# Audio tower on one core: attention scores issued round the column groups, states as four 32x32 products, moments on GpSimd, levels by halves, and a new order

## The chip, the cores and the metric

One NeuronCore of a Trainium2 chip runs the whole program. The metric is the device time of one execution in microseconds. The engines are PE (TensorE, matrix products), DVE (VectorE), ACT (ScalarE), POOL (GpSimd) and SP (SyncE, which here only issues DMAs). Everything is fp32.

## The reference, cut to what matters

```python
h = dct(frames(x))                                   # 16 batches x 938 tokens x 128
def attn(x):                                         # lam = exp(-exp(time_decay)), 4 heads of 32
    h = layernorm(x)*g + b;  xx = shifted(h)
    q, k, v, gate = four mixes of (h, xx), each @ W.T
    q, k = exp(rmsnorm(q)), exp(rmsnorm(k))
    A_t = lam*A_{t-1} + k_t v_t^T;  z_t = lam*z_{t-1} + k_t
    att = sigmoid(gate) * (q_t A_t / q_t.z_t) @ Wo.T;  x = x + att
    return x + gelu(layernorm2(x) @ W1.T) @ W2.T
h = h + attn(layernorm(h))
def ffn(x):                                          # expert of batch b is b % 8
    xa = layernorm(x)*g + b;  xa = xa @ attn_w.T + attn_b + x
    return gelu((gelu(xa @ fc1[e].T + b1) @ fc2[e].T + b2) @ next_w.T + next_b)
h = h + ffn(layernorm(h))
```

## The kernel before, in words

A batch has 938 tokens, in 8 tiles of 128 (the last has 42, of which two windows of 32 are computed). Work that fits 512 columns goes by halves: g=0 is tiles 0 to 3, g=1 tiles 4 to 7 (426 columns). Each engine has its own program, a fixed order of steps written out by hand in its `body`; engines meet only at semaphores, and each engine takes its steps strictly in that order. `every_round` calls `body` for B + LAST rounds; `at(late)` gives the batch that a round works on with a lateness, so that `at(0)` is the newest batch and `at(1)`, `at(2)` the ones before it. Products go to eight PSUM banks: five are shared by a list of uses (`USES`, with each use's lateness), and `BETWEEN`, `DIAG` and `SOUT` are held for the attention.

The linear attention with decay is computed in chunks. Within a tile the scores of a query and a key are a product of q and k, each scaled by powers of lam against a common reference point, and this is done by levels, so that no power grows large. `qlev` (L711) writes three scaled copies of q per group g of 256 columns into `qq` (Q8: inside 32, Q32: second half of each 64, Q64: second half of each 128). `inside` (L833) writes eight scaled copies `ki` of k, and `between` (L836) three copies `ko` and two `kw`; both go through `klevels` (L820 to L829), one DVE instruction per copy and group (L827). `spread` (L307) moves `qq` by DMA into the block form `qx`, where each head's rows are kept apart and the rest are zero. A score product thus has 128 rows, 32 stationary columns (keys of one window) and moves 4 heads x n columns.

On PE, per tile c:
- `pairs_a` (L976) fills bank BETWEEN: for each window w the three `ko` products (L990, 4x8 = 32 columns moved), then the two `kw` products of 32 keys (L994, 128 columns), then one with 64 keys (L998, 256 columns).
- `pairs_b` (L1001) fills bank DIAG: for each of 8 positions j, round the windows, one `ki` product (L1014, 16 columns).
- `scan` (L1018) adds in bank SOUT the state that enters the tile (L1029, one full 128x128 product with `ab`, the four heads' states on the diagonal of a block matrix) and the tile's own part (L1033, four products of 32 stationary columns, one per head).

An fp32 product is issued as two PE instructions, each with its own weight load (PEld), so counts of the profile are twice those of the code. The window w, and in L1033 the head, choose the 32 output partitions and thereby the group of 32 columns of the PE array.

ACT copies bank BETWEEN into `px` (`pxs`, L514); DVE then lays the masked bank DIAG over it (`merge`, L756, L763), which `scan` multiplies. `chain` (L752) scans the states `af` on DVE, and POOL's `states` (L393) multiplies them with the head mask into `ab`. Bank and buffer reuse binds them: `pairs_a(c+1)` waits for `pxs(c)`, `pairs_b(c+1)` for `merge(c)`.

The three layer norms are `stats` (L641, DVE), `gathered` (L644 to L647, bn_aggr per tile), a scaling of the variance (L653, L654, L782), a power on POOL (L386, L403, L412), and a normalising pass per tile on DVE (L672, L788, L808). `powq` (L391) is POOL's root for the norms of q and k.

The steps around a batch: `samples`, `dcts`, `hcopy`, norm 1, `nTs`, `hlT`, `shifted`, `mixes`, `qkv`, `squares`, `sums`, `norms`, `tokens`, `qkTs`, `exps`, levels, pairs, `scan`, `gated` (needs `gz`, which `hand_gate` brings by DMA), `attends`, `attended`, norm 2, `n2Ts`, `w1s`, `gelu1` (L533), `w2s` (L1056), `hidden`, norm 3, `nmTs`, `n1Ts`, `ats`, `x_attn`, `f1s` (L1078), `gelu2` (L553), `f2s` (L1084), `fin`, `oTs`, `result`, `store`.

Of the kernel before, what the change touches and what calls it, by code (L numbers as in the profile page):

```python
# [6 lines left out]
ALU = mybir.AluOpType  # L7
# [3 lines left out]
P = 128  # L11
HEADS = 4
# [15 lines left out]
LAST = 2  # L28
USES = [
# [23 lines left out]
def program(nc, A, out):  # L53
# [15 lines left out]
    with ctx:  # L69
# [42 lines left out]
        st1, vv1 = sb("st1", TILES, 6), sb("vv1", TILES, 2)  # L112
        hl = sb("hl", PADT + 1)
# [21 lines left out]
        ab = sb("ab", NST, P)  # L135
# [35 lines left out]
        bn1 = sem("bn1"); ag1 = sem("ag1"); var1 = sem("var1"); nl_ok = sem("nl_ok"); d_ok = sem("d_ok")  # L171
# [5 lines left out]
        x2_ok = sem("x2_ok"); bn2 = sem("bn2"); ag2 = sem("ag2"); var2 = sem("var2"); nl2_ok = sem("nl2_ok")  # L177
        h1_ok = sem("h1_ok"); bn3 = sem("bn3"); ag3 = sem("ag3"); var3 = sem("var3"); nb3_ok = sem("nb3_ok"); n1_ok = sem("n1_ok")
# [3 lines left out]
        t_ok = sem("t_ok"); ab_ok = sem("ab_ok"); kin_ok = sem("kin_ok"); kon_ok = sem("kon_ok")  # L182
# [87 lines left out]
        def _(sp):  # L270
# [927 lines left out]
```

## Time and profile before

| | us |
|---|---|
| median of 3 runs | 1221.79 (1215.12 to 1226.37) |
| the profiled execution | 1218.9 |
| its span | 1217.1, granted clock 0.990 |
| PE busy | 1138.9 (94%) |
| DVE busy | 986.5 (81%) |
| ACT busy | 621.5 (51%) |
| POOL busy | 300.9 (25%) |

The span runs from the first to the last instruction of the profiled execution. A PE instruction counts as busy from its start until its result is written, so closely packed small products overlap in time, and the drain between two of them counts as busy too. What a stretch of PE costs is therefore better read from the starts of its rows.

### The profile page before, as it was taken

The page shows a single profiled execution, that of the slowest core. Times are in us where ns is not written, and L with a number is a line of the kernel's source. Part 1 is how long each engine was busy: PE and PEld are TensorE (multiplying, and loading weights), DVE is VectorE, ACT ScalarE, POOL GpSimd, SP SyncE. Part 2 cuts the span into 40 slices and gives each one's busy share as a digit, 9 for nine tenths or more (in the row PEclk, how much of TensorE's full clock was granted, in tenths as well). Part 3 has the DMA queues.
Part 4 walks back from the last instruction along what each step waited for, and adds up shares of the span by engine and source line. Part 5 has one row for each costly group of instructions (what it writes and reads, how often), then busy time and mean ns, then how long its engine had stood idle before and what let it go on. Part 6 is the DMA issues. An engine that isn't in the chain of part 4 may idle for free.

```text
span 1217.1 us, 43497 instructions
## 1 busy us (share of the span) xinstructions
PE 1138.9 (94%) x17955; PEld 807.8 (66%) x17955; DVE 986.5 (81%) x3362; ACT 621.5 (51%) x1100; POOL 300.9 (25%) x174
## 2 busy tenths in 40 slices
PE   4799999999999999999999999999999999999997
PEld 4576676666767676766666667666676766667664
DVE  7878788797887979788796887979879797987962
ACT  3346446363554736446363554736446364554634
POOL 4123131221403223131311403223131221403211
PEclk8799999999999999999999999999999999999999
DMA  5321313222141312313222141312313222141210
GB/s 188 106 64 39 113 43 110 65 79 56 43 132 44 87 47 66 110 43 113 63 78 55 44 130 46 88 45 63 112 44 110 63 80 57 43 132 45 87 55 17
DMA packets 51492, 91.48 MB, mean 75 GB/s; under 512 B 9536, under 2 KB 26592, under 8 KB 51296
## 3 DMA queue, kind: packets, MB, share of 16 engines
q1 hardware_dynamic: 51296, 88.69, 24.1%
q8 instruction: 144, 2.36, 0.8%
q14 instruction: 52, 0.43, 0.1%
HBM read 19.50 MB, written 9.78 MB: 24 GB/s over the span
## 4 chain that ended last, share of the span: by engine, by line
PE 83%; DVE 9%; POOL 4%; issue 3%; ACT 2%; DVEq 0%; POOLq 0%
PE bank L1056 10%; PE bank L1049 9%; PE bank L1084 9%; PE bank L1078 8%; PE bank L919 8%; PE bank L914 7%; PE bank L1014 7%; PE bank L998 5%; PE bank L990 4%; PE bank L1033 4%; POOL nrm L391 3%; PE bank L1029 3%; PE bank L954 3%; PE bank L943 2%; PE bank L994 2%
## 5 line engine op out<-in xcount | busy, mean ns | idle before, releaser
L514 ACT ACTIVATE px<-bank 128x512 f32<-128x512 f32 (+1 forms) x128 | 72.8, 569 | 218.0 <-PE bank L998 152.9
L763 DVE COPY_PREDICATED px<-mask,bank 128x512 f32<-128x512 uint32 (+1 forms) x128 | 88.6, 692 | 79.6 <-issue 76.8
L1078 PE MATMUL bank<-xa,f1w 128*128 128x512 f32 (+1 forms) x256 | 124.7, 587 | 14.8 <-DVE qtok L704 13.0
L1056 PE MATMUL bank<-w,hid 128*128 128x128 f32 x1024 | 121.9, 277 | 17.2 <-ACT hid L533 17.2
L1056 PEld LDWEIGHTS bank<-w,hid 128*128 128x128 f32 x1024 | 116.7, 192 | 31.6 <-ACT hid L533 31.6
L1014 PEld LDWEIGHTS bank<-qx,ki 128*32 128x32 f32 x7680 | 89.6, 110 | 42.3 <-issue 33.9
L827 DVE TENSOR_TENSOR ki<-k,rp 128x96 f32<-128x96 f32 (+13 forms) x512 | 113.2, 295 | 0.6 <-ACT k L499 0.6
L397 POOL TENSOR_TENSOR ab<-af,heads 128x896 f32<-128x896 f32 x16 | 40.8, 2552 | 291.1 <-DVE af L755 291.1
L1049 PE MATMUL bank<-c,w 128*128 128x512 f32 (+1 forms) x256 | 111.4, 568 | 1.1 <-ACT c L527 0.9
L1084 PE MATMUL bank<-hid,f2w 128*128 128x512 f32 (+1 forms) x256 | 107.5, 563 | 0.0
L1014 PE MATMUL bank<-qx,ki 128*32 128x16 f32 x7680 | 99.2, 193 | 6.9 <-issue 6.6
L408 POOL TENSOR_TENSOR t_sum<-x,hs 128x512 f32<-128x512 f32 x32 | 51.4, 1605 | 214.2 <-DVE x L775 200.8
L391 POOL TENSOR_TENSOR nrm<-ssq,phalf 128x8 f32<-128x8 f32 x32 | 66.6, 2082 | 149.7 <-DVE ssq L691 149.7
L553 ACT ACTIVATE hid<-bank,f1b 128x512 f32<-128x512 f32 (+1 forms) x128 | 81.4, 650 | 40.6 <-PE bank L1078 40.3
L533 ACT ACTIVATE hid<-bank 128x512 f32<-128x512 f32 (+1 forms) x128 | 71.9, 562 | 51.4 <-PE bank L1049 51.4
L990 PE MATMUL bank<-qx,ko 128*32 128x32 f32 x2880 | 79.6, 199 | 3.0 <-issue 2.7
L386 POOL TENSOR_TENSOR hs<-vv,nhalf 128x16 f32<-128x16 f32 x16 | 46.4, 2900 | 127.8 <-DVE vv L654 127.8
L1078 PEld LDWEIGHTS bank<-xa,f1w 128*128 128x128 f32 x256 | 39.8, 189 | 55.8 <-DVE qtok L704 25.4
L686 DVE SCALAR_TENSOR_TENSOR mixed<-d,vec,hl 128x938 f32<-128x938 f32 x64 | 76.0, 1188 | 0.6
L412 POOL TENSOR_TENSOR rr<-vv,nhalf 128x8 f32<-128x8 f32 x32 | 52.4, 1636 | 90.8 <-DVE vv L654 90.8
L990 PEld LDWEIGHTS bank<-qx,ko 128*32 128x32 f32 x2880 | 68.2, 111 | 10.0 <-issue 8.8
L1084 PEld LDWEIGHTS bank<-hid,f2w 128*128 128x128 f32 x256 | 46.2, 190 | 42.1 <-issue 42.1
(142 smaller groups left out, 2414.0 us busy)
## 6 DMA issues: line engine op xcount, KB each, us to landing
qx<-qq SPq DMA_DIRECT2D x256, 96.0 KB
hs<-hs SPq DMA_DIRECT2D x32, 532.0 KB, 4.4
v<-v_f SPq DMA_DIRECT2D x16, 512.0 KB, 3.9
gz<-gate_f SPq DMA_DIRECT2D x16, 512.0 KB, 4.7
xT<-in_xT SPq DMA_DIRECT2D x16, 468.5 KB, 4.0
f1w<-in_fc1T SPq DMA_DIRECT2D x16, 256.0 KB, 2.7
f2w<-g_dram SPq DMA_DIRECT2D x16, 256.0 KB, 3.0
out<-t_sum SPq DMA_DIRECT2D x16, 256.0 KB, 2.7
```

The costliest lines, as they stand in the source:

```text
L391: gp.tensor_tensor(nrm[:, i, :], ssq[:, i, :], phalf[:, :], ALU.pow).then_inc(rr_ok[i], 1)
L553: nc.scalar.activation(hid[:, j, cols(g)], bk(f"f1_{g}{j}")[:, 0:width[g]], ACT.Gelu, bias=f1b[:, b % E, j:j + 1]).then_inc(ge2, 1)
L763: V.copy_predicated(px[c % 2][0:n, :, 0:n], mask[0:n, 0:n].rearrange("p (o m) -> p o m", o=1).to_broadcast([n, HEADS, n]), bank[DIAG][0:n, ...
L827: last = V.tensor_tensor(view(dst[:, GRP * (g % 2):GRP * (g % 2) + w]), view(k[:, GRP * g:GRP * g + w]), over(rp[:, P - ref:P - ref + n], ...
L914: last = mm(dst[:, P * i:P * i + P], src[:, P * m:P * m + P], w[:, :], start=True, stop=True)
L919: last = nc.tensor.transpose(dst[:, P * i:P * i + P], src(m), ident[:, :])
L990: last = mm(O[r, :, WIN * w + t:WIN * w + t + EIGHT], ko[:, j - 1, k0 + WIN * w:k0 + WIN * w + WIN], x[:, :, Q8 + t0 + t:Q8 + t0 + t + EIG ...
L1014: last = mm(D[WIN * w:WIN * w + WIN, :, WIN * w + j:WIN * w + WIN:EIGHT], ki[:, j, k0 + WIN * w:k0 + WIN * w + WIN], x[:, :, t0 + j:t0 + W ...
L1049: mm(dst[:, 0:width[g]], w1[:, P * j:P * j + P], c1[:, cols(g)], start=True, stop=True).then_inc(w1_ok, 1)
L1056: last = mm(dst[:, P * i:P * i + P], hid[:, j, P * m:P * m + P], w2[:, j, :], start=(j == 0), stop=(j == 3))
L1078: mm(dst[:, 0:width[g]], f1w[:, P * j:P * j + P], xa[:, cols(g)], start=True, stop=True).then_inc(f1_ok, 1)
L1084: last = mm(dst[:, 0:width[g]], f2w[:, P * j:P * j + P], hid[:, j, cols(g)], start=(j == 0), stop=(j == 3))
```

## The change

1. `pairs_a` and `pairs_b` become one step `pairs`. The product with 64 keys is two with 32 keys, each 256 columns; the `kw` products come first, then the `ko` products round the windows (w inside j), then `ki` as before. The step waits for both `pxs(c-1)` and `merge(c-1)` at its start.
2. The block matrix `ab` and POOL's `states` go. `scan` multiplies each head's 32x32 state with that head's 32 rows of `qc`: four products per tile on the array's diagonal.
3. The aggregation of the moments and the scaling of the variance leave DVE; POOL does them with six to eight small instructions and waits between them.
4. `qlev`, `inside` and `between` run on 512 columns instead of 256, half as many instructions.
5. LAST is 3, the list of bank uses is new, and the order of every engine's body is new: the round begins in the middle of the batch that was at(0), so that most of the attention is now at(1) and the feed-forward part at(2).

```diff
-LAST = 2
+LAST = 3
...
+        def last_pairs(eng, b, g):
+
+            if g:
+                eng.wait_ge(pb_ok, nth(b, TILES, TILES // 2))
+            else:
+                before(eng, pb_ok, b, TILES, TILES)
...
             def spread(b, g):
-                sp.wait_ge(ql_ok, nth(b, GROUPS, g + 1))
+                sp.wait_ge(ql_ok, nth(b, 2, g // 2 + 1))
...
+            def moments(st, mv, sums, odd, s, up, n):
+
+                gp.tensor_tensor(sums[:, s, :], st[:, s, 1:3], st[:, s, 4:6], ALU.add)
+                gp.tensor_tensor(odd[:, s], st[:, s, 1], st[:, s, 4], ALU.subtract).then_inc(up, 1)
+                gp.wait_ge(up, n + 1)
+                gp.tensor_tensor(odd[:, s], odd[:, s], odd[:, s], ALU.mult)
+                gp.tensor_scalar(mv[:, s, 0], sums[:, s, 0], 0.5, None, ALU.mult).then_inc(up, 1)
+                gp.wait_ge(up, n + 2)
+                gp.tensor_scalar(odd[:, s], odd[:, s], 32.0, None, ALU.mult).then_inc(up, 1)
+                gp.wait_ge(up, n + 3)
+                gp.tensor_tensor(odd[:, s], odd[:, s], sums[:, s, 1], ALU.add).then_inc(up, 1)
+                gp.wait_ge(up, n + 4)
+
+            def twice_normed(vv, odd, s, up, n):
+
+                gp.tensor_scalar(vv[:, s, 0], odd[:, s], 1.0 / P, EPS, ALU.mult, ALU.add)
+                gp.tensor_scalar(vv[:, s, 1], odd[:, s], (1.0 + EPS) / P, EPS * EPS, ALU.mult, ALU.add).then_inc(up, 1)
+                gp.wait_ge(up, n)
+
             def pow1(b):
-                gp.wait_ge(var1, nth(b, 1, 1))
+                all_ = slice(0, TILES)
+                gp.wait_ge(bn1, nth(b, 2, 2))
+                before(gp, hs1_in, b, 16, 16)
+                moments(st1, mv1, sm1, od1, all_, mo1, nth(b, 5, 0))
+                twice_normed(vv1, od1, all_, mo1, nth(b, 5, 5))
...
-            def states(b):
...
-            def gathered(mv, st, ms, ag, count):
...
             def qlev(b, g):
-                dve.wait_ge(eq, nth(b, 2, g // 2 + 1))
+                dve.wait_ge(eq, nth(b, 2, g + 1))
...
+                    last = V.tensor_tensor(qq[:, 2 * g:2 * g + 2, at:at + GRP * n // m].rearrange("p o (x m) -> p o x m", m=n),
+                                           q[:, 2 * g:2 * g + 2, :].rearrange("p o (x m) -> p o x m", m=m)[:, :, :, skip:m],
...
             def klevels(b, g, parts, done):
-                last_use(dve, b, g)
+                last_pairs(dve, b, g)
-                    w = scan_w[g] if m <= WIN else GRP
+                    w = HALF if m > WIN else min(HALF, WINS * WIN - HALF * g)
...
-            def pairs_a(b, c):
+            def pairs(b, c):
...
                 if c % 2 == 0:
                     pe.wait_ge(qx_in[g % 2], nth(b, 128, 64 * (g // 2 + 1)))
+                    pe.wait_ge(kon_ok, nth(b, 2, c // 4 + 1))
                 if c:
                     pe.wait_ge(px_ok, nth(b, TILES, c))
                 else:
                     before(pe, px_ok, b, TILES, TILES)
                 if c % 2 == 0:
+                    pe.wait_ge(kin_ok, nth(b, 2, c // 4 + 1))
+
+                if n == NW:
+                    t0 = Q64 + P // 2 * o
+                    for w in (0, 1):
+                        r = slice(WIN * w, WIN * w + WIN)
+                        mm(O[r, :, P // 2:P], kw[:, 1, k0 + WIN * w:k0 + WIN * w + WIN], x[:, :, t0:t0 + P // 2], start=True, stop=True)
+                for w in range(0, n, 2):
+                    t0 = Q32 + P // 2 * o + WIN * (w // 2)
+                    mm(O[WIN * w:WIN * w + WIN, :, WIN * w + WIN:WIN * w + 2 * WIN], kw[:, 0, k0 + WIN * w:k0 + WIN * w + WIN],
+                       x[:, :, t0:t0 + WIN], start=True, stop=True)
+                for j in range(1, NE):
+                    for w in range(n):
+                        t0 = P * o + WIN * w + EIGHT * j
+                        last = mm(O[WIN * w:WIN * w + WIN, :, WIN * w + EIGHT * j:WIN * w + EIGHT * j + EIGHT],
+                                  ko[:, j - 1, k0 + WIN * w:k0 + WIN * w + WIN], x[:, :, Q8 + t0:Q8 + t0 + EIGHT], start=True, stop=True)
+                last.then_inc(pa_ok, 1)
...
             def scan(b, c):
-                    pe.wait_ge(ab_ok, nth(b, 1, 1))
+                    pe.wait_ge(af_ok, nth(b, 1, 1))
...
-                    mm(S[:, s0:s0 + n], ab[:, c - 1, :], qc[:, P * c:P * c + n], start=True, stop=False, skip_group_check=True)
+                    for hd in range(HEADS):
+
+                        r = slice(HD * hd, HD * hd + HD)
+                        mm(S[r, s0:s0 + n], af[r, c - 1:HD * NST:NST], qc[r, P * c:P * c + n], start=True, stop=False, skip_group_check=True)
```

The new bodies, step by step (steps without a mark belong to the batch at(1), those in round brackets to at(0), those in square brackets to at(2)); a digit behind a step is its half, its part or its tile:

- PE: nTs 1, [w2s 0], q 0, [n2Ts 1], q 1, [w1s 1 0 to 1 2], k 0, [w1s 1 3], k 1, [w2s 1, nmTs 0], qkTs q 0, v 0, qkTs q 1, [n1Ts 0], qkTs k 0, [ats 0], gates 0, qkTs k 1, [f1s 0 0], v 1, [f1s 0 1 to 0 3], pairs 0, [f2s 0], pairs 1, us, [nmTs 1, n1Ts 1], scan 0, pairs 2, scan 1, (dcts 0), pairs 3, gates 1, zts, scan 2, (dcts 1), scan 3, rTs 0, rTs 1, [ats 1], pairs 4, [f1s 1 0 to 1 2], pairs 5, attends 0, [f1s 1 3], scan 4, [oTs 0], pairs 6, [f2s 1], pairs 7, scan 5, n2Ts 0, scan 6, scan 7, w1s 0 0, w1s 0 1, attends 1, w1s 0 2, w1s 0 3, (nTs 0), [oTs 1].
- DVE: mixes 1, sums q 0, sums q 1, mixes 2, [normed3 0], sums k 0, norms q, sums k 1, tokens q 0, tokens q 1, mixes 3, [hidden 1], norms k, tokens k 0, tokens k 1, qlev 0, [x_attn 0], between 0, inside 0, [stats3 1], from_start, decayed, merge 0, [normed3 1], zscan, merge 1, chain, zmul, merge 2, qlev 1, inside 1, denominators, merge 3, between 1, gate 0, gate 1, [x_attn 1], merge 4, gated 0, merge 5, attended 0, stats2 0, (stats1 0, stats1 1), merge 6, normed2 0, merge 7, [result 0], gated 1, (normed), attended 1, stats2 1, [result 1], (shifted, mixes 0), normed2 1, hidden 0, stats3 0.
- POOL: powq q, [resid 1], powq k, [pow3 1], pow2 0, (pow1), resid 0, pow2 1, pow3 0.
- SP: [hand_h2, spread 2, spread 3, hand_gate], store 0 and 1 of at(3), [expert], spread 0, (samples), hand_h1, spread 1, hand_v.
- ACT: its steps are moved to match; tanhs 1 now stands behind gelu2 of half 0 and ahead of pxs 3.

## Rows read from the trace of the kernel before

**Rows 1.** Page: busy time and share of each engine, instructions
```profile
PE 1138.9 (94%) x17955; PEld 807.8 (66%) x17955; DVE 986.5 (81%) x3362; ACT 621.5 (51%) x1100; POOL 300.9 (25%) x174
```

**Rows 2.** Windows: length, PE, PEld, DVE, ACT, POOL busy, clock, DMA share
```profile
78.60:151.60 73.00, 69.59 (x1114) 49.14 (x1115) 61.01 (x212) 39.18 (x68) 18.27 (x11) 1.00 0.21 64
...
1100.00:1173.00 73.00, 71.06 (x1161) 50.42 (x1163) 60.85 (x211) 38.59 (x69) 18.20 (x10) 1.00 0.22 67
1173.00:1217.10 44.10, 35.19 (x174) 21.40 (x174) 15.01 (x55) 18.27 (x33) 5.51 (x4) 1.00 0.10 28
```

**Rows 3.** Waits of PE from 151.6 to 1100 us: total, times, longest
```profile
PE bank L1056 <- ACT hid L533: 13.6, 26, 0.7
PE bank L1078 <- DVE qtok L704: 11.3, 13, 0.9
PE bank L1014 <- issue: 5.3, 7, 1.3
PE bank L990 <- issue: 2.5, 5, 0.9
```

**Rows 4.** Timeline of PE, one tile's pairs: start, us, engine, line
```profile
630.82 0.56 PE L990 MATMUL bank<-qx,ko 128*32 128x32 f32 x21
...
631.32 0.28 PE L994 MATMUL bank<-qx,kw 128*32 128x128 f32 x2
631.53 0.65 PE L998 MATMUL bank<-qx,kw 128*64 128x256 f32 x2
632.10 0.98 PE L1072 MATMUL bank<-c,wat 128*128 128x426 f32 x2
633.02 0.72 PE L1014 MATMUL bank<-qx,ki 128*32 128x16 f32 x62
633.56 0.20 PE L990 MATMUL bank<-qx,ko 128*32 128x32 f32 x1
```

**Rows 5.** Timeline of PE, full products of 512 columns
```profile
624.32 3.60 PE L1084 MATMUL bank<-hid,f2w 128*128 128x512 f32 x8
```

**Rows 6.** Timeline of PE, two scans
```profile
651.28 0.49 PE L1029 MATMUL bank<-qc,ab 128*128 128x128 f32 x2
651.70 0.42 PE L1033 MATMUL bank<-px,v 128*32 128x128 f32 x8
651.94 0.73 PE L1014 MATMUL bank<-qx,ki 128*32 128x16 f32 x62
...
655.50 0.39 PE L1029 MATMUL bank<-qc,ab 128*128 128x128 f32 x2
655.82 0.42 PE L1033 MATMUL bank<-px,v 128*32 128x128 f32 x8
```

**Rows 7.** Groups of DVE by form: busy, mean ns, idle before
```profile
L827 DVE TENSOR_TENSOR ki<-k,rp 128x128 f32<-128x128 f32 x48 | 13.6, 284 | 0.0
L827 DVE TENSOR_TENSOR ki<-k,rp 128x256 f32<-128x256 f32 x48 | 20.0, 418 | 0.0
L647 DVE BATCH_NORM_AGGREGATE mv<-st 128x2 f32<-128x6 f32 x256 | 24.0, 156 | 2.7
L782 DVE TENSOR_SCALAR vv<-mv 128x4 f32<-128x4 f32 x32 | 5.9, 185 | 1.1
```

**Rows 8.** Groups of POOL: busy, mean ns, idle before
```profile
L408 POOL TENSOR_TENSOR t_sum<-x,hs 128x512 f32<-128x512 f32 x32 | 51.4, 1605 | 214.2 <-DVE x L775 200.8 <-DMA out<-t_sum 13.4
L397 POOL TENSOR_TENSOR ab<-af,heads 128x896 f32<-128x896 f32 x16 | 40.8, 2552 | 291.1 <-DVE af L755 291.1
L375 POOL MEMSET phalf<- 128x8 f32 x1 | 0.1, 104 | 0.0
```

**Rows 9.** Timeline of POOL and DVE beside each other
```profile
606.02 1.97 POOL L408 TENSOR_TENSOR t_sum<-x,hs 128x512 f32<-128x512 f32 x1
606.78 1.23 DVE L806 SCALAR_TENSOR_TENSOR nb<-mv,rr 128x4 f32<-128x4 f32 x1
...
614.61 2.53 POOL L391 TENSOR_TENSOR nrm<-ssq,phalf 128x8 f32<-128x8 f32 x1 [6.62 <-DVE ssq L691]
619.57 1.64 POOL L391 TENSOR_TENSOR nrm<-ssq,phalf 128x8 f32<-128x8 f32 x1 [2.44 <-DVE ssq L691]
```

**Rows 10.** DMA issues: engine, count, KB each, median us to landing
```profile
gz<-gate_f SPq DMA_DIRECT2D x16, 512.0 KB, 4.7
```

More of the change, by code:

```diff
@@ L354, in body @@
             def body(at):
+                if (b := at(2)) is not None:
+                    hand_h2(b); spread(b, 2); spread(b, 3); hand_gate(b)
+                if (b := at(3)) is not None:
+                    store(b, 0); store(b, 1)
+                if (b := at(2)) is not None:
+                    expert(b)
                 if (b := at(1)) is not None:
-                    spread(b, 0); spread(b, 1); hand_v(b)
+                    spread(b, 0)
                 if (b := at(0)) is not None:
@@ L376, in _ @@
             gp.memset(zq[:, :], 1.0)
+            gp.memset(hs0[:, SH:], 0.0)
             for tile in (hl, mixed[0], mixed[1]):
@@ L1092, in body @@
             def body(at):
+                if (b := at(1)) is not None:
+                    nTs(b, 1)
+                if (b := at(2)) is not None:
+                    w2s(b, 0)
+                if (b := at(1)) is not None:
+                    qkv(b, "q", 0)
+                if (b := at(2)) is not None:
+                    n2Ts(b, 1)
+                if (b := at(1)) is not None:
+                    qkv(b, "q", 1)
+                if (b := at(2)) is not None:
+                    w1s(b, 1, 0); w1s(b, 1, 1); w1s(b, 1, 2)
@@ new lines, in body @@
+                if (b := at(1)) is not None:
+                    qkv(b, "k", 0)
+                if (b := at(2)) is not None:
+                    w1s(b, 1, 3)
+                if (b := at(1)) is not None:
+                    qkv(b, "k", 1)
+                if (b := at(2)) is not None:
+                    w2s(b, 1); nmTs(b, 0)
+                if (b := at(1)) is not None:
+                    qkTs(b, 0, 0); qkv(b, "v", 0); qkTs(b, 0, 1)
+                if (b := at(2)) is not None:
+                    n1Ts(b, 0)
@@ L1095, in body @@
                 if (b := at(1)) is not None:
-                    pairs_b(b, 7); n2Ts(b, 0); scan(b, 6); scan(b, 7); w1s(b, 0, 0); w1s(b, 0, 1); attends(b, 1)
+                    pairs(b, 3); gates(b, 1); zts(b); scan(b, 2)
+                if (b := at(0)) is not None:
+                    dcts(b, 1)
+                if (b := at(1)) is not None:
+                    scan(b, 3); rTs(b, 0); rTs(b, 1)
+                if (b := at(2)) is not None:
+                    ats(b, 1)
+                if (b := at(1)) is not None:
+                    pairs(b, 4)
@@ new lines, in body @@
+                if (b := at(2)) is not None:
+                    f1s(b, 1, 0); f1s(b, 1, 1); f1s(b, 1, 2)
+                if (b := at(1)) is not None:
+                    pairs(b, 5); attends(b, 0)
+                if (b := at(2)) is not None:
+                    f1s(b, 1, 3)
+                if (b := at(1)) is not None:
+                    scan(b, 4)
+                if (b := at(2)) is not None:
+                    oTs(b, 0)
+                if (b := at(1)) is not None:
+                    pairs(b, 6)
@@ L1097, in body @@
+                if (b := at(2)) is not None:
+                    f2s(b, 1)
+                if (b := at(1)) is not None:
+                    pairs(b, 7); scan(b, 5); n2Ts(b, 0); scan(b, 6); scan(b, 7); w1s(b, 0, 0); w1s(b, 0, 1); attends(b, 1)
                     w1s(b, 0, 2); w1s(b, 0, 3)
+                if (b := at(0)) is not None:
+                    nTs(b, 0)
                 if (b := at(2)) is not None:
                     oTs(b, 1)
-                if (b := at(1)) is not None:
-                    w2s(b, 0); n2Ts(b, 1)
```

331 lines of the change are left out of this document (132 added, 199 removed), and 10 rows, old and new, of the table USES.

## The prediction

> **What bounds it.** I read the page first: PE is busy 94% of the span, DVE 81%, the others far less [rows 1]. That names PE, but a busy share counts drains, so I then cut the span at the first DCT product of each batch. From 78.6 to 1173.0 us there are 15 such rounds, 1094.4 / 15 = 72.96 us each, all at full clock; the reader is to see that first and last of them look alike, with DVE at 61 us and ACT at 38 to 39 of 73 [rows 2]. Before them lie 78.6 us of fill, after them 44.1 us of drain. Third, PE's waits inside 13 of the rounds: 13.6 for gelu, 11.3 for the root on the way to the first expert product (put down to qtok), 5.3 and 2.5 unnamed at the pairs: 32.7 / 13 = 2.5 us a round [rows 3]. So a round is 70.5 us of PE work and 2.5 of waits: what PE issues sets the time, and only 2.5 us a round can come from the order alone. Last I read the starts in one tile of pairs and in two scans [rows 4, 6].
>
> **Prices on PE.** 512 columns take 0.43 us: eight in 3.60 with a tail [rows 5]. That is 0.84 ns a column, so 0.107 us for 128, 0.215 for 256, 0.027 for 32. In L1033 eight products of 128 columns, two per column group, are through in 651.94 - 651.70 = 0.24 us, hardly over 2 x 0.107: the four groups run beside each other, and the second of a group does not hold up the rest [rows 6]. In L1014 64 instructions take 633.56 - 633.02 = 0.54 us, 8.5 ns each, 34 ns per group [rows 4]. A change of tile shape costs about 0.10: L1029 takes 0.32 to the next start where the array was already in the full shape, 0.11 over its 2 x 0.107, and 0.42 where it came from the narrow one, since a second weight load then lies open too [rows 6].
>
> **Pairs.** Before: L990 to the product after L998 is 632.10 - 630.82 = 1.28 us, with two changes of shape in it (32 to 64 keys, and out), so 1.08 without; L1014 adds 0.54: 1.62 [rows 4]. L990 comes in runs of six per group, 21 of them in 0.56 - 0.20 us, 18 ns each, so about two groups at a time. After: the first column group has the longest chain, two of 256 (0.43), two of 128 (0.21), six of 32 at about 0.03 (0.18), 0.82 in all, then 0.54 of L1014: 1.36. The others fit beside it. Gain 0.26 a tile. Bounds: 0.26 is the end above, since the first group cannot do with less; were every instruction to start only after the one before it, the 0.82 would be about 0.86, and with ten open weight loads of some 10 ns 0.96, so 0.12 is the end below. I take 0.26, as L1033's row shows just this pattern. Seven tiles: 1.8 us a round; the last tile has no 64-key product and two windows, and stays as it is.
>
> **Changes of shape.** Going through PE's order step by step I count 35 a round before and 34 after: the seven 32-to-64 changes go, but each pair step then leaves the narrow shape once more, and L990 and L1014 share one entry. 0.1 us.
>
> **States.** Before, per tile from 1 on, 0.42 or 0.32 with the change out; by the step ahead of it four and three of the seven, 2.64 a round. After: eight instructions on four 32x32 places, two deep, 2 x 0.107 + 0.03 + the change out 0.10 = 0.34, 2.4 a round. Gain 0.25. No row shows an array cut by rows, so the bounds are wide: 0.34 if the diagonal runs beside itself as column groups do, 8 x 0.107 + 0.10 = 0.96 if not (a loss of 4.1 a round). I take the first, by the nearest row, L1033. POOL's 2.55 us for `ab` [rows 8] leave the way from `chain` to scan 1, which had cover.
> The Trainium skill (TensorEngine Tiling (Array Packing), Gotcha 1) says that different row tiles cannot write one PSUM bank at the same time, and all four states go to bank SOUT. By that rule the four would have to follow each other, and the sum would be 1257; no row before has two row tiles, so the trace can't say. It is a rival below.
>
> **Other engines.** DVE: 24 aggregations at 24.0 / 256 = 0.09 us and some 14 small scalings and memsets leave, about 3.6 a round; levels on 512 columns save one start each, 2 x 284 - 418 = 150 ns, for 26 + 6 fewer instructions 4.8 a round [rows 7]. DVE falls from 61 to about 53 of 70.6 us. It is not the bound by sum, but PE waits for it at places. POOL: 38 small instructions come a round. A line through 512 and 896 elements (1605 and 2552 ns) gives 2.5 ns an element and 0.34 us at none; the memset of 8 says 0.10 as the end below, and 0.9 more when DVE is at work is the end above (2.53 against 1.64 for the same root) [rows 8, 9]. I take 0.34, the line's own. A norm's moments take 8 x 0.34 + 5 waits of about 0.1 = 3.2 us in place of some 0.75 on DVE: each of five norm groups comes 2.5 us later. POOL is then busy some 29 of 70 us. ACT: the same work; `tanhs` 1 now lies behind a gelu, which may add two table loads where there are about 33 us free; I take nothing. SP: the same DMAs. `spread` 2 and 3 now stand behind `hand_h2` and ahead of `hand_gate`, and `spread` 1 behind the loads of the next batch; the data of each is done some 4 us or more ahead of its pair step by my walk. LAST = 3 adds a nineteenth round, but that holds only what the eighteenth lost.
>
> **Waits.** I walked through the new order with the durations above. The gelu waits (1.0 a round) go: qkv k 1 now lies ahead of w2s 1, and nTs 1 and others ahead of w2s 0. The wait at the first expert product (0.9) shrinks, as more steps stand ahead of it. What is late next: qkTs k 0 for the root and `hidden` 1 queued ahead on DVE; pairs 0 for `between` and `inside`, now 512 columns before the first pair, about 1 us; `attends` 0, since `gated` 0 needs the DMA of the gate, 4.7 us behind `gate` 1 [rows 10], and merge 5 is queued behind it; n2Ts 0 behind POOL's moments. `pairs` now waits for both copies of the tile before, but 1.4 to 4 us of other PE work lies between most pairs against about 1 us for the merge. The walk gives 3 to 4 us, and such a walk by means errs high, since buffered steps even out. I take 2.3, about as before.
>
> **Sum.** Work 1.8 + 0.1 + 0.25 = 2.15, waits 0.2: 2.35 a round, 70.6 us. 15 rounds: -35. Fill and drain: one batch alone has nothing to cover latencies, so norm 1 costs 2.5 more, the first half of levels 2.6 more (8 + 5 instructions over 512 columns and not 256), drain 1, less 2 for the cheaper pairs: +4. Span 1217.1 - 35 + 4 = 1186; with the 1.8 around the span 1188, against 1218.9 for the profiled execution. That one lies 2.9 under the median of the three runs, which spread over 11; I leave that out and take 1187.
>
> **Rivals.**
> A. POOL's moments hold the queue (slower side). DVE takes its steps in order, so `normed2` 0 ahead of merge 7 and `normed3` 0 ahead of the norms of q and k stop everything behind them, and PE with it. For it: POOL and DVE do hold each other up; a DVE instruction on 4 elements took 1.23 us and ended as POOL's addition ended, and the same root took 0.9 us longer beside DVE [rows 9]. Against: the new instructions are tiny, and POOL is free most of the time. If four of the eight small ones are held 0.9 each, 3.6 us, at one group a round that has no cover: 1187 + 16 x 3.6 = 1245. It decides from 2.3 us of added wait a round.
> B. The diagonal products don't run beside each other: 16 x (4.1 + 0.25) = 70 more, 1257. For: nothing in this trace shows row tiles. Against: column groups do overlap, and their outputs are on different partitions.
> C. The gain turns into waits. The critical chain is PE almost throughout but DVE is at 61 of 73 us; if the chain over DVE, ACT and POOL has the same length as now, PE only waits more: about 1215. Against: DVE loses 8 us a round.
> D. The waits nearly go, 1.0 a round: 1187 - 16 x 1.3 = 1166. For: DVE is lighter and the new order spreads feed-forward steps of the batch before between the pairs.
>
> **Chances.** Forecast 0.46, D 0.18, C 0.16, A 0.12, B 0.08. This kernel's runs tell about 1% (12 us) from no change. Faster by over 1%: forecast and D, with the better part of C, 0.67; within 1%: 0.14; slower: 0.19. The likeliest case's own range is 1170 to 1205. The range 1150 to 1245 takes in D with better luck, C and A up to its price.
>
> **What would show it.** Per tile, from the first kw product to the end of L1014's successor about 1.36 us, with the 256-column products of two column groups starting within 10 ns of each other; four state products starting 7 ns apart and 0.34 from scan's start to L1033's successor in kind (0.96 for B); round 70.6 us; small POOL instructions at 0.34 (over 0.8 for A); waits of PE near 2.3 a round, at pairs 0, attends 0 and qkTs k 0. Wrong: a round over 72.5, PE waits over 5 us a round, or waits of DVE for `rr` in front of merges.

## The result and the profile after

Slower. The kernel after took 1264.1 us (median of 4 runs, 1261.2 to 1264.3) against 1220.0 for the kernel before in the same runs (4, 1215.1 to 1226.4): ratio 1.035, 95% interval 1.030 to 1.041. The forecast was 1187, with a range of 1150 to 1245.

The page of the kernel after, its parts 1 and 4, stands against [rows 1]; part 4 is the chain of work that ended last, for the kernel after and then for the kernel before:

```profile
span 1262.2 us, 44913 instructions
PE 1134.1 (90%) x18851; PEld 810.6 (64%) x18851; DVE 911.7 (72%) x2258; ACT 623.3 (49%) x1100; POOL 443.3 (35%) x767
PE 45%; DVE 27%; POOL 17%; issue 9%; DMA 1%; ACT 1%; SPq 1%; DVEq 0%; POOLq 0%
PE 83%; DVE 9%; POOL 4%; issue 3%; ACT 2%; DVEq 0%; POOLq 0%
```

PE's share fell from 94 to 90%, and DVE is 75 us less busy. The last two rows are the ones to learn from: in the kernel before the chain was 83% PE, 9% DVE and 4% POOL. Now 44% of it is DVE and POOL. PE does a little less work, and it no longer sets the time alone.

Windows of the kernel after: 14 rounds, two single ones, then a short stretch at the lower clock (columns as in [rows 2], the last one GB/s):

```profile
64.80:1116.00 1051.20, 966.60 (x16415) 689.89 (x16411) 781.75 (x1959) 537.09 (x947) 382.19 (x658) 0.99 0.24 71
587.40:663.00 75.60, 70.39 (x1178) 50.05 (x1174) 55.82 (x141) 38.53 (x68) 27.44 (x47) 0.98 0.23 71
663.00:739.80 76.80, 70.44 (x1179) 50.03 (x1175) 57.10 (x143) 38.55 (x68) 27.43 (x47) 0.98 0.23 70
669.10:672.50 3.40, 3.40 (x29) 2.41 (x26) 2.09 (x6) 3.40 (x8) 0.00 (x0) 0.50 0.51 118
```

A round is 1051.20 / 14 = 75.1 us, against 72.96 before [rows 2] and 70.6 forecast. DVE is at 782 / 14 = 55.8 us a round, which is 4.8 less than before where 8.4 less was forecast, and POOL is at 27.3 (forecast 29). Neither is the bound by its sum, so these misses don't explain the round. Outside the 15 rounds of this length the span has 1262.2 - 15 x 75.08 = 136 us, before 122.7: fill and drain grew by 13.

Waits of PE in 13 rounds, 138.2 to 1116 us (total, times, longest), against [rows 3]:

```profile
PE bank L937 <- DVE qtok L727: 15.7, 13, 1.2
PE bank L937 <- DVE nl L808: 13.9, 12, 1.2
PE bank L987 <- issue: 9.6, 5, 2.5
PE bank L937 <- ACT x L570: 8.6, 8, 1.1
PE bank L937 <- DVE ktok L731: 7.9, 12, 0.7
PE bank L1031 <- issue: 6.6, 9, 1.6
```

L937 are the transposes: 46.1 / 13 = 3.5 us a round there, which wait for DVE's and ACT's normed rows and tokens. The waits for gelu are gone, as forecast. What DVE itself waits for, in the same stretch:

```profile
DVE tick L784 <- ACT px L546: 75.2, 49, 3.7
DVE nb L824 <- POOL rr L442: 70.9, 26, 3.1
DVE nl L808 <- POOL rr L430: 14.6, 12, 1.2
```

The first row is slack at the merges; e5, the version below with the moments back on DVE, has 73.2 us of it too. `rr` is the root that POOL delivers behind its moments: DVE stands 70.9 / 26 = 2.7 us at each half of norm 3, with everything queued behind it, in all (70.9 + 14.6) / 13 = 6.6 us a round.

One such chain, norm 3 half 0, in the timeline of POOL and DVE (start, us, engine, line; in brackets the idle time ahead), and behind it the start of the next one, half 1:

```profile
628.66 1.08 POOL L394 TENSOR_TENSOR sm<-st 128x8 f32<-128x8 f32 x1 [2.74 <-DVE st L681]
629.70 0.20 POOL L395 TENSOR_TENSOR od<-st 128x4 f32<-128x4 f32 x1
...
630.86 1.17 POOL L402 TENSOR_TENSOR od<-od,sm 128x4 f32<-128x4 f32 x1
...
632.66 1.67 POOL L442 TENSOR_TENSOR rr<-vv,nhalf 128x8 f32<-128x8 f32 x1
630.79 1.19 DVE L709 SCALAR_TENSOR_TENSOR mixed<-d,vec,hl 128x938 f32<-128x938 f32 x1
634.36 0.16 DVE L824 SCALAR_TENSOR_TENSOR nb<-mv,rr 128x4 f32<-128x4 f32 x1 [2.39 <-POOL rr L442]
...
650.88 2.10 POOL L394 TENSOR_TENSOR sm<-st 128x8 f32<-128x8 f32 x1 [11.18 <-DVE st L681]
650.72 1.21 DVE L761 TENSOR_TENSOR qc<-qq,pw 128x1024 f32<-128x1024 f32 x1
651.84 1.08 DVE L745 TENSOR_TENSOR kcT<-kcT,to_end 128x896 f32<-128x896 f32 x1
656.64 0.16 DVE L824 SCALAR_TENSOR_TENSOR nb<-mv,rr 128x4 f32<-128x4 f32 x1 [3.06 <-POOL rr L442]
```

The statistics ended at about 628.5, the root began at 632.66: 4.1 us. The same form of instruction takes 0.20 us, or 1.08 to 1.17, or 2.10. L402 began 0.07 us after DVE's full-width mix at L709 and ended with it; L394 of half 1 lasted through two DVE instructions, L761 and L745. Another chain, norm 2 at 682.5 with no hold, needs 1.9 us from the first instruction to the root. Held instructions are common; the groups of POOL by line, of the whole span:

```profile
L394 POOL TENSOR_TENSOR sm<-st 128x8 f32<-128x8 f32 (+1 forms) x80 | 59.0, 738 | 685.7 <-DVE st L681 685.7
L402 POOL TENSOR_TENSOR od<-od,sm 128x4 f32<-128x4 f32 (+1 forms) x80 | 40.4, 505 | 6.7
L428 POOL TENSOR_SCALAR vv<-od 128x4 f32<-128x4 f32 x32 | 18.5, 580 | 2.8
```

Over 0.2 us each, these three groups hold 43 + 24 + 12 = 79 us in 80 chains: 1.0 us a chain, and a chain takes 3.1 us on average. But the holds are not spread evenly. From the first instruction to the root, norm 1 takes 2.3 us and is never held. Norm 2 takes 1.9 in one half and, in 14 of 16 batches, 3.7 in the other. Norm 3, the one that DVE waits for longest, is held in 30 of its 32 chains, by 1.7 to 1.9 us, and takes 3.9 to 4.1 then for 2.15 free. All 73 held instructions ended 0.05 to 0.06 us after a DVE instruction did. The Trainium skill (GPSIMD Engine Reference, section 2, Architecture) says that GpSimd has one read port for SBUF and shares it with VectorE; these rows agree with it in kind, and the size, 0.9 to 1.9 us on an instruction of 4 or 8 columns, is from the rows.

PE's timeline, one tile's pairs and one scan, against [rows 4, 6]:

```profile
650.16 0.41 PE L1015 MATMUL bank<-qx,kw 128*32 128x256 f32 x2
650.18 0.41 PE L1018 MATMUL bank<-qx,kw 128*32 128x128 f32 x2
...
650.81 0.33 PE L1023 MATMUL bank<-qx,ko 128*32 128x32 f32 x17
650.97 0.80 PE L1031 MATMUL bank<-qx,ki 128*32 128x16 f32 x63
651.70 3.70 PE L1104 MATMUL bank<-hid,f2w 128*128 128x512 f32 x8
...
662.28 0.45 PE L1049 MATMUL bank<-qc,af 32*32 32x128 f32 x8
662.66 0.43 PE L1053 MATMUL bank<-px,v 128*32 128x128 f32 x8
```

The tile is 651.70 - 650.16 = 1.54 us with 0.10 of change of shape in it, so 1.44 (forecast 1.36, before 1.62). The states take 662.66 - 662.28 = 0.38 (forecast 0.34; one after another they would take 0.96).

### The profile page after: what moved, and what is told of

It is laid out like the page before. It is cut to its first block, busy times and chain, and to the rows that moved or that the text cites. A ratio compares the mean times of both kernels' runs of the same rounds, so it can differ in the third digit from the quotient of the medians.

```text
span 1262.2 us, 44913 instructions
## 1 busy us (share of the span) xinstructions
PE 1134.1 (90%) x18851; PEld 810.6 (64%) x18851; DVE 911.7 (72%) x2258; ACT 623.3 (49%) x1100; POOL 443.3 (35%) x767
## 4 chain that ended last, share of the span: by engine, by line
PE 45%; DVE 27%; POOL 17%; issue 9%; DMA 1%; ACT 1%; SPq 1%; DVEq 0%; POOLq 0%
PE bank L1104 5%; PE bank L932 5%; PE bank L1098 5%; PE bank L1031 5%; PE bank L937 4%; POOL sm L394 3%; POOL rr L442 3%; PE bank L1053 3%; PE bank L1049 3%; PE bank L1015 3%; DVE nl L695 3%; DVE st L681 3%; POOL od L402 3%; DVE ki L845 3%; DVE nl L826 2%
## 5 line engine op out<-in xcount | busy, mean ns | idle before, releaser
L394 POOL TENSOR_TENSOR sm<-st 128x8 f32<-128x8 f32 (+1 forms) x80 | 59.0, 738 | 685.7 <-DVE st L681 685.7
L845 DVE TENSOR_TENSOR ki<-k,rp 128x448 f32<-128x448 f32 (+14 forms) x256 | 93.5, 440 | 30.2 <-PE bank L1031 30.2
L1098 PE MATMUL bank<-xa,f1w 128*128 128x512 f32 (+1 forms) x256 | 112.6, 564 | 1.7 <-DVE xa L832 0.9
L1031 PEld LDWEIGHTS bank<-qx,ki 128*32 128x32 f32 x7680 | 93.4, 109 | 12.6 <-issue 12.5
L1018 PE MATMUL bank<-qx,kw 128*32 128x128 f32 x480 | 95.3, 281 | 1.8 <-DVE px L785 1.8
L570 ACT ACTIVATE x<-t_sum,nb,rr 128x128 f32<-128x128 f32 x128 | 52.7, 482 | 78.3 <-DVE nb L824 76.4
L937 PE MATMUL bank<-ident,nl 128*128 128x128 f32 x384 | 61.4, 284 | 30.1 <-DVE nl L808 17.6
L1015 PE MATMUL bank<-qx,kw 128*32 128x256 f32 x448 | 71.3, 393 | 11.6 <-DVE px L785 10.1
L709 DVE SCALAR_TENSOR_TENSOR mixed<-d,vec,hl 128x938 f32<-128x938 f32 x64 | 75.9, 1188 | 0.6
L937 PEld LDWEIGHTS bank<-ident,nl 128*128 128x128 f32 x384 | 44.2, 144 | 47.7 <-issue 34.2
L1023 PE MATMUL bank<-qx,ko 128*32 128x32 f32 x2880 | 72.5, 201 | 0.0
L1104 PEld LDWEIGHTS bank<-hid,f2w 128*128 128x128 f32 x256 | 46.1, 189 | 40.5 <-issue 39.4
L784 DVE MEMSET tick<- 128x1 f32 x128 | 7.6, 59 | 89.1 <-ACT px L546 89.1
```

The costliest lines, as they stand in the source:

```text
L394: gp.tensor_tensor(sums[:, s, :], st[:, s, 1:3], st[:, s, 4:6], ALU.add)
L845: last = V.tensor_tensor(view(dst[:, 0:w]), view(k[:, HALF * g:HALF * g + w]), over(rp[:, P - ref:P - ref + n], w // m, n), ALU.mult)
L937: last = nc.tensor.transpose(dst[:, P * i:P * i + P], src(m), ident[:, :])
L1015: mm(O[r, :, P // 2:P], kw[:, 1, k0 + WIN * w:k0 + WIN * w + WIN], x[:, :, t0:t0 + P // 2], start=True, stop=True)
L1018: mm(O[WIN * w:WIN * w + WIN, :, WIN * w + WIN:WIN * w + 2 * WIN], kw[:, 0, k0 + WIN * w:k0 + WIN * w + WIN], x[:, :, t0:t0 + WIN], start= ...
L1031: last = mm(D[WIN * w:WIN * w + WIN, :, WIN * w + j:WIN * w + WIN:EIGHT], ki[:, j, k0 + WIN * w:k0 + WIN * w + WIN], x[:, :, t0 + j:t0 + W ...
```

## The experiments

Each kernel ran in the same job as the kernel before, in three jobs (e1 to e4, e5 to e8, e9 to e12). The kernel before differs by up to 4 us between them, so times of different jobs are compared by their ratios. Medians and ratios (95%):

| | us | before | ratio |
|---|---|---|---|
| e1_pairs | 1224.0 | 1220.8 | 1.002 [1.000, 1.004] |
| e2_states | 1231.2 | 1220.8 | 1.007 [1.004, 1.010] |
| e3_pairs_states | 1234.5 | 1220.8 | 1.011 [1.007, 1.015] |
| e4_moments | 1273.5 | 1220.8 | 1.042 [1.039, 1.046] |
| e5_after_dve | 1205.9 | 1220.5 | 0.987 [0.984, 0.991] |
| e6_after_dve_block | 1208.7 | 1220.5 | 0.990 [0.986, 0.993] |
| e7_after_dve_groups | 1201.5 | 1220.5 | 0.985 [0.981, 0.989] |
| e8_after_block | 1288.6 | 1220.5 | 1.054 [1.049, 1.059] |
| e9_before_short | 1169.7 | 1224.5 | 0.956 [0.952, 0.959] |
| e10_pairs_short | 1157.1 | 1224.5 | 0.946 [0.942, 0.951] |
| e11_norm1_pool | 1207.8 | 1224.5 | 0.988 [0.983, 0.992] |
| e12_old_products | 1242.4 | 1224.5 | 1.015 [1.010, 1.019] |

To compare them I split each trace's rounds. The round is the mean of 14 (15 for before). PE idle is what PE waits in one. The clock term is half of the time at 0.5, per round. What is left is PE's work. Stalls are the gaps of over 0.3 us, from start to start, between two products of 32 stationary columns on the same line (8.5 ns apart when they flow), over the whole span:

| | round | PE idle | clock | work | stalls, us (times) |
|---|---|---|---|---|---|
| before | 72.96 | 2.98 | 0 | 69.98 | 17.4 (22) |
| after | 75.08 | 6.04 | 0.85 | 68.2 | 25.0 (19) |
| e1 | 73.33 | 4.71 | 0.85 | 67.8 | 42.8 (38) |
| e2 | 73.73 | 3.11 | 0.6 | 70.0 | 21.2 (25) |
| e3 | 73.65 | 5.04 | 0.5 | 68.1 | 55.5 (48) |
| e4 | 76.28 | 5.39 | 0.5 | 70.4 | 23.7 (24) |
| e5 | 71.64 | 2.99 | 1.1 | 67.6 | 34.4 (28) |
| e6 | 71.49 | 3.23 | 1.0 | 67.3 | 21.3 (23) |
| e7 | 71.15 | 2.63 | 0.6 | 67.9 | 24.1 (26) |
| e8 | 76.83 | 7.21 | 1.9 | 67.7 | 10.4 (13) |
| e9 | 69.75 | 2.21 | 0.2 | 67.3 | 0.6 (1) |
| e10 | 68.86 | 3.43 | 0.1 | 65.3 | 8.5 (8) |
| e11 | 71.36 | 2.78 | 0.7 | 67.9 | 27.6 (23) |
| e12 | 73.74 | 3.40 | 0.4 | 70.0 | 23.6 (19) |

### One part alone, in the old order

**e1_pairs**: the kernel before with the new sequence of products.

```diff
-                for w in range(n):
-                    for j in range(1, NE): ... ko product of window w ...
-                for w in range(0, n, 2): ... kw, 32 keys ...
-                    last = mm(O[0:P // 2, :, P // 2:P], kw[:, 1, k0:k0 + P // 2], ...)
+                    for w in (0, 1): ... kw, two times 32 keys, 256 columns ...
+                for w in range(0, n, 2): ... kw, 32 keys ...
+                for j in range(1, NE):
+                    for w in range(n): ... ko ...
```

> The kernel before, with the products of pairs_a in the new sequence and the 64-key product as two of 32 keys; nothing else. Theory P (the PE part of the forecast holds, and the loss lies elsewhere): a pairs_a step falls from 1.28 us to about 1.0, 7 tiles x 16 batches x 0.26 = 29 us, time about 1191. Rival O (PE was no longer the bound, whatever it saves turns into waits): within 1% of before, above 1208.

Measured +3 us, the interval at no change. The 1191 of theory P missed, and the time is where rival O had it; but PE's part did come, as the work of a round fell by 2.2 us. The idle time rose by 1.7 and the clock took 0.85, so more than all of it was lost again. Where PE waits, in the whole span:

```profile
PE bank L1015 <- issue: 23.0, 26, 2.7
PE bank L969 <- issue: 9.4, 6, 2.1
```

and in the timeline, one of these inside a run of 16-column products:

```profile
712.31 0.71 PE L1015 MATMUL bank<-qx,ki 128*32 128x16 f32 x54
715.72 0.27 PE L1015 MATMUL bank<-qx,ki 128*32 128x16 f32 x9 [2.70 <-issue]
715.87 0.69 PE L969 MATMUL bank<-v_f,kcT 128*32 128x32 f32 x56
```

Nothing releases it: no semaphore stands between the 54th and the 55th product. What fits is the supply of instructions, though no run changed the supply itself. The DMA records of PE's instruction queue (queue 8) show packets of 16384 bytes. One landed at 714.36, 1.36 us ahead of the restart at 715.72. Part 3 of the page counts them (packets, MB, share), here of the kernel before, of e1 and of the kernel after:

```profile
q8 instruction: 144, 2.36, 0.8%
q8 instruction: 145, 2.38, 0.8%
q8 instruction: 151, 2.47, 0.8%
```

PE ran 17955 instructions before, and as many weight loads: some 250 of the 35910 to a packet. No two packets start less than 3.23 us apart in any of the kernels. 128 narrow products with their loads, one packet, are through in 1.1 us. So a run of several hundred outruns the supply, and the denser e1 packs them, the sooner it does: 43 us of such stalls against 17. In every kernel the restarts come 1.2 to 1.6 us after a landing (once 1.1).

**e2_states**: the kernel before, with the states by head in `scan` and without `ab`; **e3_pairs_states**: e1 and e2 together.

```diff
-                    mm(S[:, s0:s0 + n], ab[:, c - 1, :], qc[:, P * c:P * c + n], ...)
+                    for hd in range(HEADS):
+                        r = slice(HD * hd, HD * hd + HD)
+                        mm(S[r, s0:s0 + n], af[r, c - 1:HD * NST:NST], qc[r, P * c:P * c + n], ...)
```

> The kernel before, with the states as four 32x32 products per tile and without POOL's block matrix; nothing else. Theory P: 0.25 us a round less on PE and 2.5 us less latency between chain and scan 1: 1212 to 1219. Rival (the 32x32 shape costs more than it saves, by its changes of shape or by weights read at a stride of 28 bytes): above 1225.

> Both PE edits on the kernel before, everything else as before. Theory P: the two gains add, about 1186. Rival O: above 1208. A second rival (denser products leave PE less active, and the granted clock falls inside the steady rounds as it does in the changed kernel): about 1200, with the clock below 0.985.

Measured +10 and +14: theory P missed in both. e2 is where its rival had the time, above 1225, but not for the rival's reason. The work did not change for the states (70.0 in e2 for 69.98), and of the 0.77 us that its round is longer the clock has 0.6. In e3 the stalls rose to 55.5 us, the idle time by 2.1 a round, and the clock took 0.5. In the old order both edits of PE together are a small loss of 1.1%.

**e4_moments**: the kernel before with POOL's `moments`, and the aggregation and scalings taken off DVE, in the old order.

```diff
-            def gathered(mv, st, ms, ag, count): ...      # DVE, with variance scalings
+            def moments(st, mv, sums, odd, s, up, n): ... # POOL, with its waits
             def pow2(b, g):
+                moments(st2, mv2, sm2, od2, ...)
```

> The kernel before, with the moments on POOL and the aggregation gone from DVE; order and all else as before. Theory M (the way from bn_stats over POOL's six to eight small instructions to the power is what costs the changed kernel its time): norms come 2.5 to 5 us later at places with no cover, 1250 to 1300, with DVE waiting for rr. Rival O (the order and the merged pairs cost it): within 1% of before, since DVE loses 3.6 us a round and POOL has time.

Measured +52.7 us: this part alone is dearer than the whole change. Waits of DVE in its rounds, 79.1 to 1147 us:

```profile
DVE nb L817 <- POOL rr L444: 53.4, 28, 2.7
DVE nl L801 <- POOL rr L432: 48.3, 29, 2.4
```

Over 7 us a round, and PE's idle time is up by 2.4. This run also tells length from holding. No chain of norm 2 is held here: they take 1.9 or 2.2 us from the first instruction to the root, and still DVE waits 48.3 / 29 = 1.7 us for each. So the length alone costs time where the next step in DVE's queue wants the answer.

### The change with a part taken back

**e5_after_dve**: the kernel after with the moments on DVE again; **e6_after_dve_block**: e5 with the block matrix; **e7_after_dve_groups**: e5 with levels in groups of 256; **e8_after_block**: the kernel after with the block matrix.

```diff
 e5                                             (from the kernel after)
-                moments(st1, mv1, sm1, od1, all_, mo1, nth(b, 5, 0))
+                gp.wait_ge(var1, nth(b, 1, 1))
...
-                    stats1(b, 0); stats1(b, 1)
+                    stats1(b, 0); stats1(b, 1); variance1(b)
 e7                                             (from e5)
-                    between(b, 0); inside(b, 0)
+                    between(b, 0); inside(b, 0); between(b, 1); inside(b, 1)
 e6, e8                                         (from e5, from the kernel after)
-                    for hd in range(HEADS): ...
+                    mm(S[:, s0:s0 + n], ab[:, c - 1, :], qc[:, P * c:P * c + n], ...)
```

> The changed kernel, with the moments back on DVE (bn_aggr and the scalings, as before); order, merged pairs, states by head and levels by halves as changed. Theory M (POOL's chain of small instructions holds DVE and through it PE): about 45 us less than the changed kernel, 1210 to 1225, and the waits of DVE for POOL's rr fall from 5 us a round to under 1. Rival O (the order itself is late at these places): above 1245.

> As e5, and the states back as one block product with POOL's mask. Theory F (PE's instruction supply: more and shorter PE instructions close together run its queue dry, and stalls end some 1.4 us after a 16 KB packet of instructions lands): 96 instructions a round fewer near the pairs, 8 to 15 us less than e5. Rival (states by head are worth their 0.25 us a round in this order): 3 to 8 us more than e5.

> As e5, and the levels of q and k in groups of 256 columns again, twice the DVE instructions. If the halves are worth their 4.8 us of DVE time a round: 10 to 40 us more than e5. If DVE has the slack since PE is the bound: within 5 us of e5.

> The changed kernel with moments on POOL as changed, and only the states back as one block product. Theory F: 5 to 15 us less than the changed kernel (1264). Theory P (the PE gain counts): 4 us more, and POOL's mask product, 2.5 us in a queue that is now late, another 5 or more.

e5 is 58 us below the kernel after and 14.7 below the one before, 4 us better than the theory's best. This settles the sign: with everything else of the change in place, the moments on POOL turn a gain of 1.3% into a loss of 3.5%. PE's waits in e5, its first three, and the window of its 14 rounds, 63.5 to 1066.5 us:

```profile
PE bank L978 <- issue: 12.9, 6, 2.8
PE bank L1022 <- issue: 7.1, 12, 1.2
PE bank L923 <- ACT c L550: 6.0, 14, 0.4
```

```profile
63.50:1066.50 1003.00, 961.02 (x16414) 690.79 (x16410) 818.35 (x2476) 537.10 (x947) 230.86 (x126) 0.98 0.25 75
```

No wait of DVE for `rr` is left among DVE's, and none of PE at the transposes over 0.5 us a round. DVE is 2.6 us a round *busier* than in the kernel after (818 against 782), and the round is 3.4 us shorter.

e6 against e5 is +2.8 us, the intervals overlap: states by head are worth little there, and the gain of 8 to 15 us from fewer instructions that the supply theory expected of e6 did not come. PE waits 12.7 us for `ab` in e6's 14 rounds and the round is no longer for it. e8 is 24 us above the kernel after, where the supply theory had it 5 to 15 below. There the mask product stands in the POOL queue that is already late, and PE waits for it:

```profile
PE bank L1055 <- POOL ab L429: 25.8, 13, 2.2
```

That wait is not the whole price: the clock takes 1.9 us a round in e8 for 0.85 in the kernel after, and seven of its fourteen falls to 0.50 come within 1.8 us behind such a wait, of 2.0 to 2.2 us each.

e7, levels in small groups again, is 4.3 us below e5, with intervals that overlap. So the levels on 512 columns are worth nothing that shows. They take 1.9 us of busy time a round off DVE (its window has 845.17 against 818.35 in 14 rounds), where the prediction had 4.8. e7 is the fastest version of all that leave nothing out: 1201.5, 1.5% under the kernel before.

### How large the supply's part is

**e9_before_short** and **e10_pairs_short** are the kernel before and e1 with the `ki` products of positions 4 to 7 left out, half of the 16-column ones.

```diff
-                for j in range(EIGHT):
+                for j in range(EIGHT // 2):
```

> The kernel before, leaving out the ki products of positions 4 to 7, half of bank DIAG's work (3840 of the 17955 PE products with their weight loads). A base for the next run. Its PE work falls by 3840 x 8.5 ns = 33 us, and by F most of its stalls at narrow products go too: 1170 to 1190.

> The same products left out, with the new sequence of the pairs as in e1. Theory F (e1's gain of 29 us was eaten by the supply of PE instructions): with a third fewer narrow instructions the queue runs dry less, and the new sequence is now worth 12 to 29 us against e9. Rival R (the way pairs, copy on ACT, merge on DVE bounds the stage, since each bank is single): the gain stays at 0 to 5 us.

With the load off the queue (114 and 115 packets for 144), e9's stalls fall from 17.4 to 0.6 us, and the new sequence, worth -3 us with all the products, is worth 1169.7 - 1157.1 = 12.5. That is the sign that supply predicts, at the low end of its size, and it is the only one of the supply theory's four numbers that came in: those for e6, e8 and e12 missed. e10 still stalls for 8.5 us:

```profile
PE bank L990 <- issue: 12.9, 15, 1.6
```

### In the new order

**e11_norm1_pool**: e7 with norm 1's moments alone on POOL. **e12_old_products**: e7 with both edits of PE undone, the block matrix in.

```diff
 e11
-                gp.wait_ge(var1, nth(b, 1, 1))
+                moments(st1, mv1, sm1, od1, all_, mo1, nth(b, 5, 0))
 e12
+            def states(b): ...
-                    for w in (0, 1): ...  (kw, ko in the new sequence, states by head)
+                    last = mm(O[0:P // 2, :, P // 2:P], kw[:, 1, k0:k0 + P // 2], ...)
```

> e7 (the changed kernel with DVE moments and levels in groups), with the moments of norm 1 alone on POOL, where several steps lie between stats1 and normed. Theory M as refined (not POOL as such costs time, but a chain of 3 us without cover): within 6 us of e7. Rival (POOL and DVE hold each other up wherever they run together): 10 us or more above e7.

> e7 with both PE edits undone inside the new order: the old sequence of products with the 64-key product, and the states as a block product. What the PE edits are worth in the new order: by the forecast's prices 2.1 us a round, 34 us more than e7, 1235; by F only part of it, 10 to 20 us more; if nothing as in the old order (e3 against before): within 5 us of e7.

e11 is 6 us above e7 by the medians and 3 by the ratios, and the intervals overlap: norm 1, with `merge` 6 and other steps between its statistics and its use, costs little or nothing; no finer word is possible. e12 is 41 us above e7 by the medians and 36 by the ratios, as the forecast's prices had it (34) and not the supply theory (10 to 20). So the two edits of PE, a loss of 1.1% in the old order, are worth 3.0% in the new one. The windows of their 14 rounds, e7 first:

```profile
61.50:1057.60 996.10, 958.15 (x16414) 688.38 (x16410) 845.17 (x2924) 535.44 (x947) 230.83 (x126) 0.99 0.25 75
```

```profile
63.50:1095.90 1032.40, 984.55 (x15630) 694.40 (x15626) 846.03 (x2924) 538.65 (x947) 278.33 (x140) 1.00 0.24 72
```

36.3 / 14 = 2.6 us a round: 2.1 of work, as the forecast had it, and 0.8 of idle time, less 0.2 of clock. Of the idle time most is e12's wait for `ab`:

```profile
PE bank L988 <- issue: 17.5, 14, 2.1
PE bank L1046 <- POOL ab L406: 11.9, 12, 1.1
```

But e6 has the same wait, and is level with e5. So nearly all of the 36 us belong to the new sequence of the pairs, and little or nothing to the states.

In the new order full-width products of the feed-forward part stand between the pairs, and they give the supply time to catch up: e7's stalls are 24.1 us and e12's 23.6, while they went from 17.4 to 42.8 in e1 and 55.5 in e3 for the same edits. That the order is the reason is the reading that fits; it was not tried with another order.

## Why the prediction was wrong

All three of its signs of being wrong came: a round of 75.1 us (over 72.5), PE waits of 6.0 (over 5), and waits of DVE for `rr`. By its own steps:

- **Pairs, shapes, states: right in sum.** Forecast a round of 70.6 less 2.3 of waits, 68.3 of work; measured 68.2. A tile 1.44 for 1.36, states 0.38 for 0.34; the 0.25 a round that the states were to bring did not show in e2's work, and e5 against e6 shows next to nothing for them in the new order. Rival B is out: four products on the diagonal of the array, all to one bank, take 0.38 and not 0.96. The rule of the Trainium skill (TensorEngine Tiling (Array Packing), Gotcha 1) would have had them one after another; in time they did not follow it, and here the measurement decides. The 10 ns for an open weight load, on which the lower bound of the pairs' gain rests, stands in no row. Whether the rule holds for row tiles on the same partitions, no run shows.
- **Other engines: the price was right on average, by luck, and wrong where it counts.** A moments chain of 3.2 us was forecast, and 3.1 is the mean. But it isn't eight instructions of 0.34: they are 0.20 each and some 2 us in all, and the rest is holding by DVE. The prediction had seen 0.9 us of it [rows 9] and put none in the sum; norm 3 has 1.8 in nearly every chain and takes 3.9. DVE's relief was forecast too large as well: 3.6 + 4.8 us a round, measured 2.6 (e5 against the kernel after) and 1.9 (e7 against e5). By e7 against e5 that cost nothing.
- **Waits: the step that failed.** "I take 2.3, about as before", while each norm chain came 2.5 us later by the step just ahead. The walk found cover for it (it named n2Ts 0 alone as late behind the moments). It treated the delay as PE's to absorb. But DVE meets it first: normed3 0 and normed3 1 stand in DVE's queue with merges and token norms behind them, so DVE stands still for 6.6 us a round, all of these come later, and 3.05 us of it reach PE, most at the transposes. Measured: 6.0 us of idle time a round for 2.3, 3.7 x 15 = 56 us of the 77 missed. Undone, in e5, the idle time is back at 2.99, which is 3.05 x 15 = 46 us of the 58 that come back.
- **Rival A was the case**, at 0.12 the second lowest of the chances. Its threshold, 2.3 us of added wait a round, was passed: 3.05 were added over e5. Its price, 1245, was too low: it had one group a round held for 3.6 us, and the rows have both halves of norm 3 held for 1.8 each, the free part of the chain on top, and norm 2 beside it. An estimate from these rows: of the 2.7 us that DVE waits at norm 3, 1.8 are holding and 0.9 the chain's own length. What I held against A, that the instructions are tiny and POOL mostly free, was no argument: a chain that another in-order engine waits for is priced by its length, holds included, not by POOL's load. "Such a walk by means errs high, since buffered steps even out" was the sentence that let it pass.
- **The clock: not in the sum.** Rows before show full clock in all rounds. The kernel after has stretches of 3.4 us at 0.50 (1.2 GHz) inside rounds, seven between 65 and 1045 us, 0.85 us a round, 13 us in all. Three of the seven came behind scans, 4-column products and pairs with no wait of PE to speak of, as at 669.10 above. The other four came within 2 us of a wait of PE of 1.2 to 2.3 us: two "issue" stalls, a wait for the rows of norm 2 (`nl`, L808) and one for `qtok`. In e1 five of seven falls came within 1.4 us of a stall of 2.0 to 2.7 us. So a part of the clock's loss seems to be the echo of waits, those for POOL among them. It is not the moments alone, since e5 has 1.1 us a round without them, and not waits alone, since e2 has four falls without a wait over 0.5 us. What sets it off stays open.
- **Fill and drain: +4 was forecast, +13 measured.** e5 and e7 have it too (135 and 132 us), e1 to e4, in the old order, do not (123 to 125): it belongs to the new order, whose nineteenth round I had costed at nothing. What share that round has was not measured.
- **Supply: missed in the rows.** [Rows 3] shows 5.3 and 2.5 us "issue" at the pairs. I called them unnamed and went on; they look like the supply. In e1 the idle time that they stand for took 1.7 us a round of the 2.2 gained, and the clock 0.85. In the new order it took less, so it matters little for the result, but much for what each part is worth.

Sum: waits 56, clock 13, fill and drain 9, work -2: 76 of the 77 us.

Open: how the loss of the moments divides between the chain's own length and its being held. The 0.9 and 1.8 us at norm 3 are a subtraction, and e4 shows only that length alone costs DVE 1.7 us at norm 2. A shorter chain on POOL was not tried, nor were the DVE instructions that hold it (L709, L761, L745) moved away from it.

## What to carry to other kernels

Before moving small work to an idle engine, look at who waits for its answer: a chain between two steps of an in-order queue delays everything behind it by the part of its length that no other step covers, however free the other engine is. So the consumer must stand later in the queue by that length, or the chain stays where it was. Read the length from a trace in which both engines run: here it was 2.15 us free and 3.9 with long DVE instructions beside it. An idle time that the profile puts down to "issue" inside a run of small products is a resource of its own; making such runs denser bought nothing here while no wide products stood between them. And test a change in its parts in the order in which they will run: the same two edits of PE lost 14 us in one order and gained 36 in another.

## What the runs showed of the hardware

- PE's instructions come in packets of 16384 bytes, none less than 3.23 us after the last in these kernels, some 250 instructions each; narrow products of 16 columns run at 8.5 ns. Longer runs stall for up to 2.8 us and resume 1.2 to 1.6 us after a packet has landed. That the packets are the cause is the reading that fits; half of the narrowest products left out took the stalls from 17.4 to 0.6 us.
- Four 32x32 products on the array's diagonal, into different partitions of one bank, run beside each other: 0.38 us with 128 columns, a change of shape included.
- POOL's instructions on 4 or 8 columns take 0.20 to 0.31 us, and 1.0 to 1.2 or, behind two long DVE instructions in a row, 2.1 (15 times); all 73 holds end 0.05 to 0.06 us after a DVE instruction. The long ones beside them are those with two inputs or more (L709, L701, L761, L745); 29 of POOL's small instructions began beside the reduction at L714 and were not held.
- The granted clock can fall to 0.50 for 3.4 us in a kernel whose PE is 90% busy: here three times behind stretches of small products without a wait, and four times behind a wait of 1.2 to 2.3 us.
